# A GRU over 256 steps: state and update gate in two halves, the last two vector steps as one scan, and the candidate's bias by a product

## The chip, the cores and the metric

The kernel runs on one core of one Trainium2 chip. The metric is the device time of one execution in microseconds (us), median of the runs. Engines: TensorE (PE; PEld is its weight load), VectorE (DVE), ScalarE (ACT), GpSimd (POOL) and SyncE (SP), which here issues the DMAs.

## The reference, cut to what matters

Four layers run one after the other over x, 8 batches x 256 steps x 512 channels: two attention layers, a GRU over the 256 steps, and a last layer with a pooled term and a layer norm. The change is in the GRU, whose step is

```python
def cell(h, x):                       # h: [8, 512]
    gi = x @ W_ih + b_ih
    gh = h @ W_hh + b_hh
    i_r, i_z, i_n = jnp.split(gi, 3, axis=-1)
    h_r, h_z, h_n = jnp.split(gh, 3, axis=-1)
    r = jax.nn.sigmoid(i_r + h_r)
    z = jax.nn.sigmoid(i_z + h_z)
    n = jnp.tanh(i_n + r * h_n)
    h_new = (1.0 - z) * n + z * h
    return (h_new, h_new)
```

The bias of the candidate's recurrent part (the last third of b_hh) stands inside the product with r, so it can't be added to gi ahead of the loop as the others are. The layer's output is x plus all the states.

## The kernel before, in words

`attention_layers` (lines 6 to 640) computes the first two layers and leaves x, channels on partitions, in the SBUF tile xT [128, 4, 256, 8]. Its engines each walk through a written plan, batch by batch; batches 2 to 6 are a hardware loop (line 235), the others are unrolled.

`recurrent_and_last_layer` (line 642) has two blocks. In the first, lines 695 to 825, SP loads the weights (698 to 703). TensorE waits for all loads (793), then computes gi for all steps in 48 groups of eight 512-column products (801), and ScalarE evicts each group with the summed bias into giT (774). The candidate's recurrent bias is left out there.

Then each engine runs a loop of 128 passes with two steps in each; the steps are called u=0 and u=1. Nothing but semaphores orders the engines. The state hT has two buffers. One step is:

- TensorE: waits until the candidate's and the update gate's banks of the step before have been turned (808, 810) and giz is there (811). It puts the z part of gi into the bank of Z by products with an identity (814: 16 products). It waits for the state: at u=1 for hT itself (816), at u=0 for the sum of hT into xT (818). Then come the products of state and W_hh (823), in the order R, N, Z: for each gate 4 chunks c of the state by 4 column blocks j, so that gate block j lands on PSUM partitions 32j to 32j+7. A source product in f32 shows as two matmul instructions in the trace, so a step has 96 for the gates and 32 for giz.
- VectorE: turns R in 32x32 blocks into SBUF (742) and adds gi (744). It turns N (747), multiplies by r (750), adds rbias (753). It turns Z (756), then h-n (758), times z (761), plus n (764), which is the new hT.
- ScalarE: sigmoid for r and tanh for n (785), sigmoid for z (787), and a copy of the next pass's gi z part into giz (789).
- GpSimd: rbias = r * bias (716), plus gi's n part (718), and xT += hT (721).

The addresses of giT and xT depend on the loop's register, so an instruction that reads them has register instructions ahead of it. The second block (line 847) starts when the first is done on all engines, and is the last layer.

Of the kernel before, what the change touches and what calls it, by code (L numbers as in the profile page):

```python
# [641 lines left out]
def recurrent_and_last_layer(nc, xT, cond, w_ih, w_hh, b_ih, b_hh, wk, wo, rowc, cols, ident_in, out):  # L642

    fp32 = mybir.dt.float32
    ALU = mybir.AluOpType
# [3 lines left out]
    D = P * C  # L653
    GATES = 3
    TB = 64
    NB = 8
    RMS_EPS = 1e-6
    with ExitStack() as ctx:
        def sb(name, shape, dt=fp32):
            return ctx.enter_context(nc.sbuf_tensor(name, shape, dt))  # L660
        def pb(name, shape, dt=fp32):
            return ctx.enter_context(nc.psum_tensor(name, shape, dt))
        def sem(name):
            return ctx.enter_context(nc.semaphore(name))
        x2v = xT[:, :, :, :].rearrange("p c (i u) b -> p c i u b", u=2)
        giz = sb("giz", [P, 2, C, B])
        identz = sb("identz", [P, P])
        hT = sb("hT", [P, 2, C, B])
        bT = sb("bT", [P, 2, GATES * C])
        bsum = sb("bsum", [P, GATES * C])  # L670
        rbias = sb("rbias", [P, 2, 2, C, B])
        trn = sb("trn", [P, GATES, P])
        tr = [trn[:, g, :].rearrange("p (c m) -> p c m", c=C)[:, :, 0:B] for g in range(GATES)]
        pre = sb("pre", [P, GATES, C, B])
        act = sb("act", [P, GATES, C, B])
        tmp = sb("tmp", [P, 3, C, B])
        ps = [pb(f"gate{g}", [P, 512]) for g in range(GATES)]
        pg = [pb(f"pg{g}", [P, 512]) for g in range(4)]
        (s_ld, s_init, s_chain, s_rb, s_gi_mm, s_gi_ev, s_h, s_acc, s_giz) = (
            sem(n) for n in ("gru_loaded", "gates_cleared", "step_product", "bias_gated", "gi_products",  # L680
                             "gi_ready", "state_ready", "state_added", "giz_ready"))

        s_ps = [sem(f"gate_products{g}") for g in range(GATES)]
        s_tr = [sem(f"gate_turned{g}") for g in range(GATES)]
        s_pre = [sem(f"gate_summed{g}") for g in range(GATES)]
        s_act = [sem(f"gate_ready{g}") for g in range(GATES)]
        R, Z, N = 0, 1, 2
        NLD = 16 * 6
        MT = GATES * C
        gru = ctx.enter_context(ExitStack())  # L690
        giT = gru.enter_context(nc.sbuf_tensor("giT", [P, T + 2, GATES * C * B], fp32))
        whh = gru.enter_context(nc.sbuf_tensor("whh", [P, C, GATES * D], fp32))
        gi4 = giT[:, :, :].rearrange("p t (g c b) -> p t g c b", g=GATES, c=C)
        gi2 = giT[:, :, :].rearrange("p (i u) (g c b) -> p i u g c b", u=2, g=GATES, c=C)
        with nc.sbuf_tensor("wih", [P, C, GATES * D], fp32) as wih, nc.Block() as block:
            @block.sync
            def _(sp):
                sp.dma_start(wih[:], w_ih).then_inc(s_ld, 16)
                sp.dma_start(bT[:, 0], b_ih).then_inc(s_ld, 16)
                sp.dma_start(bT[:, 1], b_hh).then_inc(s_ld, 16)  # L700
                sp.dma_start(hT[:, 0], cond).then_inc(s_ld, 16)
                sp.dma_start(whh[:], w_hh).then_inc(s_ld, 16)
                sp.dma_start(identz[:], ident_in).then_inc(s_ld, 16)

            @block.gpsimd
            def _(pool):
                pool.wait_ge(s_ld, NLD)

                pool.sem_inc(s_tr[N], 1)
                pool.sem_inc(s_tr[Z], 1)  # L710
                bias_n = bT[:, 1, 2 * C:].rearrange("p (c a) -> p c a", a=1).to_broadcast([P, C, B])
                with pool.Fori(0, T // 2) as i:
                    for u in range(2):

                        pool.wait_ge(s_act[R], i * 2 + (u + 1))
                        pool.tensor_tensor(rbias[:, u, 0], act[:, R], bias_n, ALU.mult).then_inc(s_rb, 1)  # L716
                        pool.wait_ge(s_rb, i * 4 + (2 * u + 1))
                        pool.tensor_tensor(rbias[:, u, 1], rbias[:, u, 0], gi2[:, bass.ds(i, 1), u, N, :, :].rearrange("p i c b -> p (i c) b"), ALU.add).then_inc(s_rb, 1)
                        pool.wait_ge(s_h, i * 2 + (u + 1))
                        xt = x2v[:, :, bass.ds(i, 1), u, :].rearrange("p c i b -> p c (i b)")  # L720
                        pool.tensor_tensor(xt, xt, hT[:, (u + 1) % 2, :, :], ALU.add).then_inc(s_acc, 1)  # L721

            @block.vector
            def _(dve):
                dve.memset(giT[:, T:T + 2, :], 0.0).then_inc(s_init, 1)
                for g in range(3):
                    dve.memset(ps[g][:, 0:P], 0.0).then_inc(s_init, 1)
                dve.wait_ge(s_ld, NLD)
                dve.tensor_tensor(bsum[:, 0:2 * C], bT[:, 0, 0:2 * C], bT[:, 1, 0:2 * C], ALU.add).then_inc(s_init, 1)
                dve.tensor_copy(bsum[:, 2 * C:], bT[:, 0, 2 * C:]).then_inc(s_init, 1)  # L730
                dve.sem_inc(s_acc, 1)
                dve.wait_ge(s_gi_ev, 4 * MT)
                with dve.Fori(0, T // 2) as i:
                    for u in range(2):
                        t = i * 2
                        now = t + (u + 1)
                        h0, h1 = hT[:, u, :, :], hT[:, 1 - u, :, :]
                        def gi(g):
                            return gi2[:, bass.ds(i, 1), u, g, :, :].rearrange("p i c b -> p (i c) b")

                        dve.wait_ge(s_ps[R], now)
                        dve.transpose(trn[:, R, :], ps[R][:, 0:P]).then_inc(s_tr[R], 1)  # L742
                        dve.wait_ge(s_tr[R], now)
                        dve.tensor_tensor(pre[:, R], tr[R], gi(R), ALU.add).then_inc(s_pre[R], 1)  # L744

                        dve.wait_ge(s_ps[N], now)
                        dve.transpose(trn[:, N, :], ps[N][:, 0:P]).then_inc(s_tr[N], 1)  # L747
                        dve.wait_ge(s_tr[N], t + (u + 2))
                        dve.wait_ge(s_act[R], now)
                        dve.tensor_tensor(tmp[:, 0], tr[N], act[:, R], ALU.mult).then_inc(s_chain, 1)  # L750
                        dve.wait_ge(s_chain, t * 3 + (3 * u + 1))
                        dve.wait_ge(s_rb, t * 2 + (2 * u + 2))
                        dve.tensor_tensor(pre[:, N], tmp[:, 0], rbias[:, u, 1], ALU.add).then_inc(s_pre[N], 1)

                        dve.wait_ge(s_ps[Z], now)
                        dve.transpose(trn[:, Z, :], ps[Z][:, 0:P]).then_inc(s_tr[Z], 1)
                        dve.wait_ge(s_act[N], now)
                        dve.tensor_tensor(tmp[:, 1], h0, act[:, N], ALU.subtract).then_inc(s_chain, 1)
                        dve.wait_ge(s_chain, t * 3 + (3 * u + 2))
                        dve.wait_ge(s_act[Z], now)  # L760
                        dve.tensor_tensor(tmp[:, 2], tmp[:, 1], act[:, Z], ALU.mult).then_inc(s_chain, 1)
                        dve.wait_ge(s_chain, t * 3 + (3 * u + 3))
                        dve.wait_ge(s_acc, t + (u + 1))
                        dve.tensor_tensor(h1, tmp[:, 2], act[:, N], ALU.add).then_inc(s_h, 1)  # L764

            @block.scalar
            def _(a):

                a.wait_ge(s_init, 6)
# [7 lines left out]
                a.wait_ge(s_gi_ev, 4 * MT)  # L777
                for u in range(2):
                    a.copy(giz[:, u], gi4[:, u, Z]).then_inc(s_giz, 1)
                with a.Fori(0, T // 2) as i:  # L780
                    for u in range(2):
                        now = i * 2 + (u + 1)
# [274 lines left out]
```

## Time and profile before

| | us |
|---|---|
| median of 3 runs (2890.47 to 2893.78) | 2892.21 |
| span of the profiled execution | 2889.4 |
| PE busy | 2099.3 (73%) |
| DVE busy | 1209.9 (42%) |
| ACT busy | 968.4 (34%) |
| POOL busy | 521.1 (18%) |

The profiled execution's time apart from its span isn't listed; its span lies 2.8 us under the median of the runs. Busy time is the sum over instructions; an instruction that waits is not busy. A busy PE is not PE at its peak, since matmuls overlap and their ends are modelled. The shares are means over stages with different limits: attention lasts up to about 1473 us of the span, the gi products from 1492 to 1661, the recurrence from 1661 to 2768, and the last layer takes the rest. In a timeline row, "idle before <-releaser" is what the engine last waited for.

### The profile page before, as it was taken

To read this page: it belongs to the slowest core of one execution; us is meant where nothing else is said; L and a number is where in the kernel's file an instruction comes from. 1 tells how busy PE (TensorE), PEld (TensorE's weight loads), DVE (VectorE), ACT (ScalarE), POOL (GpSimd) and SP (SyncE) were. 2 spreads that over 40 slices of the span, in tenths; PEclk is the share of its full clock that TensorE was granted. 3 is DMA by queue.
4 is the path that set the end of the run, shared out by engine and by line. 5 is a ranking of instruction groups with operands and counts; after the bars stand their busy time and mean duration, and the time that the engine had idled before them with its cause. 6 is when DMAs were issued, how large, how long until landed. Compare 5 with 4: busy or idle time off the path is not lost. (4 is left out here: it accounts for less than half of the span.)

```text
span 2889.4 us, 91237 instructions
## 1 busy us (share of the span) xinstructions
PE 2099.3 (73%) x38252; PEld 1231.6 (43%) x38284; DVE 1209.9 (42%) x3495; ACT 968.4 (34%) x1884; POOL 521.1 (18%) x1184
## 2 busy tenths in 40 slices
PE   1556768787786868778669977777777777777754
PEld 0122223232332223233234466666666666666631
DVE  3425435443443535344300044444444444444456
ACT  1142434344352524335122233333333333333313
POOL 4012212022222202222100011111111111111102
PEclk8687889998898989899689999999999999999977
DMA  3352423435341443530220000000000000000001
GB/s 74 43 73 60 90 34 100 58 88 78 81 74 31 101 46 88 78 85 7 68 89 0 0 1 0 0 0 0 0 0 0 0 0 0 0 0 0 0 34 58
DMA packets 51980, 111.19 MB, mean 38 GB/s; under 512 B 11985, under 2 KB 38097, under 8 KB 46049
## 3 DMA queue, kind: packets, MB, share of 16 engines
q1 hardware_dynamic: 47328, 110.03, 19.5%
q0 software_dynamic: 4608, 0.60, 0.2%
q8 instruction: 26, 0.43, 0.1%
q14 instruction: 18, 0.14, 0.0%
HBM read 80.60 MB, written 29.41 MB: 38 GB/s over the span
## 5 line engine op out<-in xcount | busy, mean ns | idle before, releaser
L823 PE MATMUL gate<-whh,hT 128*8 128x128 f32 x24576 | 718.6, 273 | 134.5 <-POOL xT L721 93.9
L823 PEld LDWEIGHTS gate<-whh,hT 128*8 128x8 f32 x24576 | 644.8, 90 | 167.1 <-POOL xT L721 110.2
L394 DVE TENSOR_REDUCE mx<-MX 128x1 f32<-128x512 f32 x768 | 494.0, 686 | 474.2 <-PE MX L524 468.9
L459 ACT ACTIVATE pr<-ST 128x1024 f32<-128x1024 f32 x384 | 373.5, 1023 | 465.2 <-PE ST L547 239.1
L524 PE MATMUL MX<-K,Q 116*128 116x512 bf16 (+1 forms) x768 | 299.2, 427 | 192.6 <-DMA Q<-d_rows 102.4
L785 ACT ACTIVATE act<-pre 128x32 f32<-128x32 f32 x512 | 118.4, 231 | 727.8 <-DVE pre L744 466.8
L742 DVE STREAM_TRANSPOSE trn<-gate 128x128 f32<-128x128 f32 x256 | 81.2, 317 | 527.4 <-PE gate L823 527.4
L524 PEld LDWEIGHTS MX<-K,Q 116*128 116x128 bf16 (+1 forms) x768 | 69.0, 99 | 466.9 <-DVE mx L394 215.3
L814 PE MATMUL gate<-identz,giz 128*8 128x32 f32 x8192 | 109.8, 193 | 143.3 <-issue 142.2
L716 POOL TENSOR_TENSOR rbias<-act,bT 128x32 f32<-128x32 f32 x256 | 61.6, 241 | 723.1 <-ACT act L785 723.1
L544 PE MATMUL ST<-Q,K 119*128 119x512 bf16 x512 | 147.1, 413 | 49.4 <-DMA Q<-nmp 49.2
L801 PE MATMUL pg<-xT,wih 128*128 128x512 f32 x384 | 167.9, 601 | 19.3 <-DMA identz<-in_ident_dram 19.3
L340 POOL TENSOR_TENSOR nmp<-nm,zero 16x128 bf16<-16x128 f32 x48 | 21.4, 445 | 877.9 <-ACT nm L476 877.9
L814 PEld LDWEIGHTS gate<-identz,giz 128*8 128x8 f32 x8192 | 84.5, 89 | 210.2 <-issue 210.2
L785 ACT ACT_TABLE_LOAD x128 | 164.2, 1283 | 9.7
L546 PE MATMUL ST<-Q,K 100*128 100x512 bf16 x256 | 105.3, 412 | 69.8 <-DMA Q<-nmp 66.8
L570 PE MATMUL AV<-pr,va 128*17 128x512 f32 x1024 | 147.3, 650 | 0.4 <-ACT pr L459 0.4
L721 POOL TENSOR_TENSOR xT<-xT,hT 128x32 f32 x256 | 64.6, 252 | 364.8 <-DVE hT L764 364.8
L801 PEld LDWEIGHTS pg<-xT,wih 128*128 128x128 f32 x384 | 74.0, 193 | 112.9 <-issue 93.1
L476 ACT ACTIVATE nm<-MX 16x128 f32<-16x128 f32 x48 | 12.8, 267 | 282.3 <-PE MX L529 282.3
L747 DVE STREAM_TRANSPOSE trn<-gate 128x128 f32<-128x128 f32 x256 | 81.2, 317 | 54.9 <-PE gate L823 54.9
L544 PEld LDWEIGHTS ST<-Q,K 119*128 119x128 bf16 x512 | 51.0, 103 | 118.3 <-issue 43.6
(141 smaller groups left out, 2193.3 us busy)
## 6 DMA issues: line engine op xcount, KB each, us to landing
Q<-d_q SPq DMA_DIRECT2D x112, 256.0 KB
K<-d_k SPq DMA_DIRECT2D x112, 256.0 KB
d_q<-piece_q SPq DMA_DIRECT2D x96, 128.0 KB
d_k<-piece_k SPq DMA_DIRECT2D x96, 128.0 KB
xin<-in_x_dram SPq DMA_DIRECT2D x8, 512.0 KB, 12.7
x<-in_x_dram SPq DMA_DIRECT2D x8, 512.0 KB, 12.5
out_dram<-sq SPq DMA_DIRECT2D x4, 1024.0 KB, 4.3
wih<-in_w_ih_dram SPq DMA_DIRECT2D x1, 3072.0 KB, 9.7
```

The costliest lines, as they stand in the source:

```text
L394: dve.reduce_max(mx[:, u, 4 * i + qb:4 * i + qb + 1], banks[0][:, :], AX.X).then_inc(mx_red[u].sem, 1)
L459: act.activation(pr[:, kc % 2, 2 * p:2 * p + 2, :], ST[:, 2 * p * T:(2 * p + 2) * T].rearrange("p (a t) -> p a t", a=2), ACT.Exp, scale=SC ...
L524: pe.matmul(banks[0][:, :], q[0:r, h, tok(qb)], k[0:r, h, :], start=True, stop=True).then_inc(mx_mm[u].sem, 1)
L544: last = pe.matmul(o, K0[0:R0 + 7, h, tok(kc)], Q0[0:R0 + 7, h, :], start=True, stop=True)
L546: pe.matmul(o, K1[0][0:R1 + 4, h, tok(kc)], Q1[0][0:R1 + 4, h, :], start=True, stop=False)
L570: last = pe.matmul(AV[r, :], v, pr[:, kc % 2, i, :], start=kc == 0, stop=kc == KC - 1)
L742: dve.transpose(trn[:, R, :], ps[R][:, 0:P]).then_inc(s_tr[R], 1)
L747: dve.transpose(trn[:, N, :], ps[N][:, 0:P]).then_inc(s_tr[N], 1)
L785: a.activation(act[:, g], pre[:, g], f).then_inc(s_act[g], 1)
L801: last = pe.matmul(pg[n % 4][:, :], wih[:, k, m * P:(m + 1) * P], xT[:, k, TB * blk:TB * (blk + 1), :].rearrange("p t b -> p (t b)"), star ...
L814: pe.matmul(ps[Z][32 * j:32 * j + B, 32 * c:32 * c + 32], giz[:, u, c, :], identz[:, 32 * j:32 * j + 32], start=c == 0, stop=False)
L823: last = pe.matmul(ps[g][32 * j:32 * j + B, 0:P], hT[:, u, c, :], whh[:, c, o:o + P], start=c == 0 and g != Z, stop=c == C - 1)
```

## The change: what it does

- The state is kept as pairs, state [128, 2 buffers, 4 chunks, 8, 2]; the state is the second of each pair. Half 0 is chunks 0 and 1, half 1 is chunks 2 and 3, each with a semaphore of its own.
- The last two vector steps (times z, plus n) become one scan per half over 32 elements. A scan carries s = by * s + plus along the row. With by = (0, z) and plus = (h-n, n) the first of a pair gives h-n and the second z*(h-n)+n.
- The update gate is computed in two halves of 64 columns, in banks of their own, double-buffered by step: its products, its turn and its sigmoid are split, and half 1 follows half 0.
- TensorE begins R and N with half 0 of the state (chunks 0 and 1 of R, then of N), and goes on with half 1 (chunks 2 and 3 of R, then of N), then Z half 0 and Z half 1. It no longer waits for the sum into xT.
- The candidate's bias enters N's bank by one 128-column product in f32r of pick and bn_rows (the bias in a high part and a rest), as the first of its accumulation. The two GpSimd operations of rbias go; VectorE adds gi's n part itself.
- giz is copied by GpSimd, two steps ahead, after the products of Z half 1, instead of by ScalarE.
- A pass of the loop has four steps (64 passes). Three small loads are added, two of them after a wait of SP for a VectorE memset; a few set-up operations and a wait of TensorE for all evictions ahead of the loop are added.

The diff, cut to its core. The lines that it removes are those of the loops in the listing above (712 to 721, 733 to 764, 778 to 789, 804 to 825); they are left out here.

```diff
...
+        state = sb("state", [P, 2, C, B, 2])
+        by = sb("by", [P, C, B, 2])
+        plus = sb("plus", [P, C, B, 2])
...
+        bn = sb("bn", [64, P])
...
+        bn_rows = sb("bn_rows", [64, P], f32r)
...
+        psz = [[pg[0], pg[1]], [pg[2], pg[3]]]
...
+        def pairs(t, a):
+            return t[:, half(a)].rearrange("p c b v -> p (c b v)")
...
+                sp.dma_start(pick_ld[:], pick_in).then_inc(s_ld, 16)
+                sp.wait_ge(s_init, 1)
+                for j in range(2):
+                    sp.dma_start(bn[32 * j:32 * j + C, :], bhn_rows).then_inc(s_ld, 16)
...
             def _(pool):
...
+                pool.wait_ge(s_gi_ev, 4 * MT)
+                for u in range(2):
+                    pool.tensor_copy(giz[:, u], gi4[:, u, Z]).then_inc(s_giz, 1)
+                with pool.Fori(0, T // U) as i:
+                    for u in range(U):
+                        q = u % 2
+                        now = i * U + (u + 1)
+                        pool.wait_ge(s_psz[1], now)
+                        pool.tensor_copy(giz[:, q], gi_at(i, u + 2, Z)).then_inc(s_giz, 1)
+                        pool.wait_ge(s_h[0], i * U + (u + 2))
+                        pool.wait_ge(s_h[1], i * U + (u + 2))
+                        xt = xv[:, :, bass.ds(i, 1), u, :].rearrange("p c i b -> p c (i b)")
+                        pool.tensor_tensor(xt, xt, state[:, 1 - q, :, :, 1], ALU.add).then_inc(s_acc, 1)
...
+                dve.sem_inc(s_acc, 2)
+                for s in s_h:
+                    dve.sem_inc(s, 1)
+                for s in (s_tr, *s_trz):
+                    dve.sem_inc(s, 2)
                 dve.wait_ge(s_gi_ev, 4 * MT)
...
+                with dve.Fori(0, T // U) as i:
+                    for u in range(U):
+                        q = u % 2
+                        t = i * U
                         now = t + (u + 1)
...
+                        h0 = state[:, q, :, :, 1]
+                        dve.wait_ge(s_ps[tR], now)
+                        dve.transpose(trn[:, R, :], psR[:, 0:P]).then_inc(s_tr, 1)
+                        dve.wait_ge(s_tr, t * 2 + (2 * u + 3))
+                        dve.tensor_tensor(pre[:, 0], tr[R], gi_at(i, u, R), ALU.add).then_inc(s_pre[tR], 1)
+                        dve.wait_ge(s_ps[tN], now)
+                        dve.transpose(trn[:, N, :], psN[:, 0:P]).then_inc(s_tr, 1)
+                        dve.wait_ge(s_tr, t * 2 + (2 * u + 4))
+                        dve.wait_ge(s_r, now)
+                        dve.tensor_tensor(tmp[:], tr[N], rg[:], ALU.mult).then_inc(s_chain, 1)
+                        dve.wait_ge(s_chain, t * 2 + (2 * u + 1))
+                        dve.tensor_tensor(pre[:, 1], tmp[:], gi_at(i, u, N), ALU.add).then_inc(s_pre[tN], 1)
+                        dve.wait_ge(s_psz[0], now)
+                        dve.transpose(trn[:, Z, 0:64], psz[0][q][:, 0:64]).then_inc(s_trz[0], 1)
+                        dve.wait_ge(s_n, now)
+                        dve.tensor_tensor(plus[:, :, :, 0], h0, plus[:, :, :, 1], ALU.subtract).then_inc(s_chain, 1)
+                        dve.wait_ge(s_chain, t * 2 + (2 * u + 2))
                         dve.wait_ge(s_acc, t + (u + 1))
...
+                        dve.wait_ge(s_z[0], now)
+                        dve.tensor_tensor_scan(pairs(state[:, 1 - q], 0), pairs(by, 0), pairs(plus, 0), 0.0, ALU.mult, ALU.add).then_inc(s_h[0], 1)
+                        dve.wait_ge(s_psz[1], now)
+                        dve.transpose(trn[:, Z, 64:128], psz[1][q][:, 0:64]).then_inc(s_trz[1], 1)
+                        dve.wait_ge(s_z[1], now)
+                        dve.tensor_tensor_scan(pairs(state[:, 1 - q], 1), pairs(by, 1), pairs(plus, 1), 0.0, ALU.mult, ALU.add).then_inc(s_h[1], 1)
...
+                with a.Fori(0, T // U) as i:
+                    for u in range(U):
+                        now = i * U + (u + 1)
+                        a.wait_ge(s_pre[tR], now)
+                        a.activation(rg[:], pre[:, 0], ACT.Sigmoid).then_inc(s_r, 1)
+                        a.wait_ge(s_pre[tN], now)
+                        a.activation(plus[:, :, :, 1], pre[:, 1], ACT.Tanh).then_inc(s_n, 1)
+                        for z in range(2):
+                            a.wait_ge(s_trz[z], i * U + (u + 3))
+                            a.activation(by[:, half(z), :, 1], tr[Z][:, half(z)], ACT.Sigmoid).then_inc(s_z[z], 1)
...
+                pe.wait_ge(s_init, 12)
+                pe.wait_ge(s_gi_ev, 4 * MT)
+                def products(bank, g, q, c, first, done, cols=slice(0, P)):
+                    for j in range(4):
+                        o = g * D + P * j
+                        last = pe.matmul(bank[32 * j:32 * j + B, 0:cols.stop - cols.start], state[:, q, c, :, 1],
+                                         whh[:, c, o + cols.start:o + cols.stop], start=first, stop=done)
+                    return last
+                with pe.Fori(0, T // U) as i:
+                    for u in range(U):
+                        q = u % 2
+                        t = i * U
                         pe.wait_ge(s_giz, t + (u + 1))
...
+                        for z in range(2):
+                            pe.wait_ge(s_trz[z], t + (u + 1))
+                            for c in range(H):
+                                for j in range(4):
+                                    pe.matmul(psz[z][q][32 * j:32 * j + B, 32 * c:32 * c + 32], giz[:, q, H * z + c, :], identz[:, 32 * j:32 * j + 32], start=c == 0, stop=False)
+                        pe.wait_ge(s_tr, t * 2 + (2 * u + 2))
+                        pe.matmul(psN[:, 0:P], pick[:], bn_rows[:], start=True, stop=False)
+                        pe.wait_ge(s_h[0], t + (u + 1))
+                        for c in range(H):
+                            products(psR, R, q, c, c == 0, False)
+                        for c in range(H):
+                            products(psN, N, q, c, False, False)
+                        pe.wait_ge(s_h[1], t + (u + 1))
+                        for c in range(H, C):
+                            last = products(psR, R, q, c, False, c == C - 1)
+                        last.then_inc(s_ps[tR], 1)
+                        for c in range(H, C):
+                            last = products(psN, N, q, c, False, c == C - 1)
+                        last.then_inc(s_ps[tN], 1)
+                        for z in range(2):
                             for c in range(C):
...
+                                last = products(psz[z][q], Z, q, c, False, c == C - 1, slice(64 * z, 64 * z + 64))
+                            last.then_inc(s_psz[z], 1)
...
```

## Rows read from the trace of the kernel before

**Rows 1.** Busy time by stretch: us, PE, PEld, DVE, ACT, POOL busy (x instructions), PEclk, DMA share, GB/s.

```profile
1661.00:2768.00 1107.00, 828.20 (x32768) 729.19 (x32768) 515.41 (x2304) 368.29 (x1154) 190.95 (x768) 1.00 0.00 0
```

**Rows 2.** Timeline of two steps: start us, us, engine, line, operation, x count [idle before <-releaser].

```profile
2201.37 2.81 PE L823 MATMUL gate<-whh,hT 128*8 128x128 f32 x96 [0.32 <-DVE hT L764]
...
2205.07 1.28 ACT L785 ACT_TABLE_LOAD   x1
2205.22 0.19 DVE L764 TENSOR_TENSOR hT<-tmp,act 128x32 f32<-128x32 f32 x1
2205.60 0.25 POOL L721 TENSOR_TENSOR xT<-xT,hT 128x32 f32 x1 [1.42 <-DVE hT L764]
...
2205.90 2.81 PE L823 MATMUL gate<-whh,hT 128*8 128x128 f32 x96 [0.70 <-POOL xT L721]
2207.03 0.32 DVE L742 STREAM_TRANSPOSE trn<-gate 128x128 f32<-128x128 f32 x1 [1.62 <-PE gate L823]
2207.49 0.19 DVE L744 TENSOR_TENSOR pre<-trn,giT 128x32 f32<-128x32 f32 x1
2207.72 0.23 ACT L785 ACTIVATE act<-pre 128x32 f32<-128x32 f32 x1 [1.36 <-DVE pre L744]
2207.90 0.32 DVE L747 STREAM_TRANSPOSE trn<-gate 128x128 f32<-128x128 f32 x1 [0.21 <-PE gate L823]
...
2208.25 0.19 DVE L750 TENSOR_TENSOR tmp<-trn,act 128x32 f32<-128x32 f32 x1
...
2208.76 0.19 DVE L753 TENSOR_TENSOR pre<-tmp,rbias 128x32 f32<-128x32 f32 x1 [0.31 <-POOL rbias L718]
2208.87 0.31 DVE L756 STREAM_TRANSPOSE trn<-gate 128x128 f32<-128x128 f32 x1
2208.98 0.23 ACT L785 ACTIVATE act<-pre 128x32 f32<-128x32 f32 x1 [1.03 <-DVE pre L753]
2209.21 0.23 ACT L787 ACTIVATE act<-trn 128x32 f32<-128x32 f32 x1
2209.24 0.19 DVE L758 TENSOR_TENSOR tmp<-hT,act 128x32 f32<-128x32 f32 x1
...
2209.28 0.42 PE L814 MATMUL gate<-identz,giz 128*8 128x32 f32 x32 [0.57 <-issue]
...
2209.54 0.19 DVE L761 TENSOR_TENSOR tmp<-tmp,act 128x32 f32<-128x32 f32 x1
2209.77 0.19 DVE L764 TENSOR_TENSOR hT<-tmp,act 128x32 f32<-128x32 f32 x1
...
2210.01 2.81 PE L823 MATMUL gate<-whh,hT 128*8 128x128 f32 x96 [0.32 <-DVE hT L764]
```

**Rows 3.** Timeline, the loop's ends: first products and last VectorE operation.

```profile
1661.37 2.84 PE L823 MATMUL gate<-whh,hT 128*8 128x128 f32 x96
...
2767.04 0.19 DVE L764 TENSOR_TENSOR hT<-tmp,act 128x32 f32<-128x32 f32 x1
```

**Rows 4.** Timeline of the last layer, two VectorE operations over 512 elements.

```profile
2790.01 0.68 DVE L879 TENSOR_TENSOR kq<-keys 64x512 f32<-64x512 f32 x1
...
2825.26 3.35 DVE L931 RECIPROCAL rs<-rs 128x512 f32<-128x512 f32 x1 [4.17 <-ACT rs L997]
```

**Rows 5.** Groups by line, 1490 to 1661 us, TensorE (line, shapes, x count, busy us, mean ns).

```profile
L801 PE MATMUL pg<-xT,wih 128*128 128x512 f32 x384 | 167.9, 601 | 19.3 <-DMA identz<-in_ident_dram 19.3
```

**Rows 6.** DMA queues in 600 to 1250 us (packets, MB, share), all that moved.

```profile
q1 hardware_dynamic: 20637, 47.09, 39.9%
q0 software_dynamic: 2304, 0.30, 0.4%
```

**Rows 7.** The page's DMA queues over the whole span, the instruction queue.

```profile
q8 instruction: 26, 0.43, 0.1%
```

**Rows 8.** Busy time by stretch, 600 to 1250 us.

```profile
600.00:1250.00 650.00, 503.53 (x2458) 196.98 (x2475) 293.15 (x535) 261.52 (x311) 135.75 (x196) 0.89 0.40 73
```

**Rows 9.** Groups by line, 600 to 1250 us, VectorE (96 of these a batch).

```profile
L394 DVE TENSOR_REDUCE mx<-MX 128x1 f32<-128x512 f32 x380 | 244.3, 686 | 211.7 <-PE MX L524 210.4
```

More of the change, by code:

```diff
@@ L676, in recurrent_and_last_layer @@
[L676 to L677 removed]
+        pre = sb("pre", [P, 2, C, B])
+        rg = sb("rg", [P, C, B])
+        tmp = sb("tmp", [P, C, B])
+        ps = [pb(f"gate{g}", [P, 512]) for g in range(3)]
         pg = [pb(f"pg{g}", [P, 512]) for g in range(4)]
[L679 to L681 removed]
@@ new lines, in recurrent_and_last_layer @@
+        R, Z, N = 0, 1, 2
+        s_ps = [sem(f"gate_products{g}") for g in (R, N)]
+        s_psz = [sem(f"update_products{a}") for a in range(2)]
+        s_tr = sem("gates_turned")
+        s_trz = [sem(f"update_turned{a}") for a in range(2)]
+        s_pre = [sem(f"gate_summed{g}") for g in (R, N)]
+        s_z = [sem(f"update_ready{a}") for a in range(2)]
+        s_h = [sem(f"state_ready{a}") for a in range(2)]
+        psR, psN = ps[0], ps[1]
+        tR, tN = 0, 1
+        NLD = 16 * 9
@@ L723, in _ @@
             @block.vector
             def _(dve):
-                dve.memset(giT[:, T:T + 2, :], 0.0).then_inc(s_init, 1)
-                for g in range(3):
-                    dve.memset(ps[g][:, 0:P], 0.0).then_inc(s_init, 1)
+                dve.memset(bn[:], 0.0).then_inc(s_init, 1)
+                dve.memset(giT[:, T:T + U, :], 0.0).then_inc(s_init, 1)
+                dve.memset(psR[:, 0:P], 0.0).then_inc(s_init, 1)
+                dve.memset(by[:], 0.0).then_inc(s_init, 1)
+                dve.memset(state[:, 1], 0.0).then_inc(s_init, 1)
@@ L746, in _ @@
[L746 to L753, printed above, removed]
@@ L776, in _ @@
                                      ACT.Identity, bias=bsum[:, m:m + 1]).then_inc(s_gi_ev, 1)
[L777 to L782, printed above, removed]
-                        for g, f in ((R, ACT.Sigmoid), (N, ACT.Tanh)):
-                            a.wait_ge(s_pre[g], now)
-                            a.activation(act[:, g], pre[:, g], f).then_inc(s_act[g], 1)
-                        a.wait_ge(s_tr[Z], i * 2 + (u + 2))
-                        a.activation(act[:, Z], tr[Z], ACT.Sigmoid).then_inc(s_act[Z], 1)
-                        a.copy(giz[:, u], gi2[:, bass.ds(i + 1, 1), u, Z, :, :].rearrange("p i c b -> p (i c) b")).then_inc(s_giz, 1)
+                with a.Fori(0, T // U) as i:
[8 more added lines that the diff above has]
+                            a.activation(by[:, half(z), :, 1], tr[Z][:, half(z)], ACT.Sigmoid).then_inc(s_z[z], 1)
             @block.tensor
```

100 lines of the change are left out of this document (30 added, 70 removed).

## The prediction

> **What bounds the kernel now.** I read the windows by stage first. The change touches the stretch from 1661 to 2768 us, 1107 of 2889 us, in which TensorE is busy for 828 us, VectorE for 515 and ScalarE for 368 [rows 1]. No engine is full, no byte moves, and the clock is granted in full. So a chain from engine to engine sets this time, and the timeline of one step shows it [rows 2]. Take T = 2205.90, the first product of a step, as zero:
>
> - +1.13 turn of R, +1.59 plus gi, +1.82 sigmoid; +2.00 turn of N, +2.35 times r, +2.86 plus rbias, +3.08 tanh, +3.34 h-n, +3.64 times z, +3.87 plus n, +4.11 next step's first product.
>
> The 96 matmuls last 2.81 with a last one of 0.273, so one starts each 26.7 ns: 0.213 us for a gate and chunk (8 matmuls), 0.853 for a gate. R turned at +1.13 is 0.853 + 0.28; N at +2.00 is 1.706 + 0.29. So N's turn is set by TensorE, and from there VectorE and ScalarE set all. R has some slack, and Z's products and turn are covered. The other step is longer: from 2201.37 to 2205.90 it takes 4.53, because L823 waits there for xT's sum (L764 at 2205.22, L721 at 2205.60, L823 at 2205.90: 0.68) and not for the state (2209.77 to 2210.01: 0.24). A pair takes 8.64, a step 4.32, and 255 of them with one step's tail make the 1105.7 us from 1661.37 to 2767.04 [rows 3].
>
> **The parts, on the path.** The unit is one step; T is now the first product on half 0.
>
> 1. TensorE doesn't wait for the sum: 0.44 at every other step, -0.22 a step. The sum moves past the next step's start; the scan waits for the one of two steps before, done long ago.
> 2. R is ready later. R's second half comes behind N's first: 6 chunks of products instead of 4, 1.28 instead of 0.853. Turn of R at +1.56, plus gi +2.02, sigmoid +2.25. N is ready at +2.00 as before, but VectorE takes it behind R's sum: +2.13, done +2.45. "Times r" now waits for the sigmoid. From ScalarE's start to VectorE's the rows show 0.26 (tanh to h-n) and 0.33 (sigmoid z to times z) [rows 2]; I take 0.30: +2.55 instead of +2.35. Cost +0.20.
> 3. rbias goes. "Plus rbias" came 0.51 after "times r", with 0.31 idle on GpSimd. The new sum reads giT, so it is a dependent VectorE operation (0.23, L761 to L764) plus register work for the address: L742 to L744 takes 0.46 where L747 to L750 takes 0.35, so 0.11. 0.34 instead of 0.51: -0.17. Sum at +2.89, tanh +3.11, h-n +3.37.
> 4. One scan for two operations. h-n to times z was 0.30, times z to plus n 0.23, plus n to product 0.24, of which 0.19 is the operation. Now the scan starts 0.30 behind h-n, +3.67; its z was turned at +3.00 beside the tanh, and its sigmoid follows the tanh at +3.34, 0.33 ahead of the scan. Its length has no row. Below: 0.19, a plain operation over 32 elements. Above: per element the reciprocal's 3.35 us for 512 [rows 4], 0.19 + 32 x 5.5 ns = 0.36. I take 0.225, since it does two dependent operations on each element and a plain one costs 1.02 ns for each (0.68 us for 512 against 0.19 for 32, rows 2 and 4): nearer to the plain row. Next step's first product: +3.67 + 0.225 + 0.05 = **+3.94**. Against 4.11 this is -0.23 + 0.03 for the scan and rounding.
> 5. Half 1 behind it: turn of Z half 1 at +3.81. It is 0.065 shorter than 0.309 (64 columns less at 1.02 ns), done +4.05; sigmoid +4.09, scan +4.42, half ready for TensorE at +4.70. That is 0.76 after the next step's start, and half 0 has work for 0.853. So it costs nothing, with 0.09 to spare; what it exceeds 0.853 by goes onto the step in full.
>
> So a step takes 3.94, against 4.32. I read from this that halving the state buys nothing (it moves R back) and that the gain comes from parts 1, 3 and 4.
>
> **Covered, at zero.** Z's 64 matmuls of 64 columns: 32 columns start each 7.3 ns (L814: 0.42 for 32, the last 0.19), 128 each 26.7, so 64 at 13.4 are 0.855 for Z as before. TensorE ends the gates at +2.56, giz at about +3.0. The bias product is one matmul 128 wide; the nearest row, with four times the columns, has 0.60 [rows 5], and there are 0.94 until +3.94. Without that cover it would cost up to 0.6 a step. Its wait, both turns of this step, ends at +2.45, ahead of the giz products. GpSimd's giz copy waits for Z half 1's products (+2.84) and has more than a step until its use; behind it in the queue is only the sum into xT, for which VectorE waits two steps later. It may meet VectorE at the SBUF (about +3.0 to +3.25, against plus gi at +2.89): between 0 and 0.1 a step; in rows 2 VectorE's operations have 0.19 beside GpSimd's too, so 0. The table load (1.28) stands behind the last sigmoid of a pass, now +4.32 to +5.60; the next sigmoid is due at 3.94 + 2.25 = +6.19.
>
> **Once.** From +4.42 instead of +3.87 in the last step, inside the sum below. giz by GpSimd and the wait for all evictions ahead of the loop: +0.3 (the copy waited for them before, too). Three loads of 32 KB and less behind identz, the last one waited for (19.3 us, rows 5): between 0 and +3, I take +1; SP's wait is for a VectorE memset at the block's start, with two small loads behind it.
>
> **The sum.** 255 x 3.94 + 4.42 = 1009.1; 1105.7 - 1009.1 = 96.6 less, 1.3 more: -95.3. The profiled execution's span of 2889.4 becomes 2794; it lies 2.8 under the median of the runs, so 2892.2 becomes **2797**.
>
> **Loading of the code, a rule against it.** A pass on TensorE grows from 512 matrix instructions (256 matmuls, 256 weight loads) to 4 x 322 = 1288. The first layers' loop shows what such a pass costs: from 600 to 1250 us TensorE ran 4933 of them [rows 8], with 380 maxima at 96 a batch [rows 9], 1246 per pass, and no packet of an instruction queue moved in four passes [rows 6], while over the span there were 26 of 16 KB [rows 7]. So a pass of this size stays loaded, and I put it at zero. The Trainium skill (Runtime: NRT & Kernel Launch, Instruction fetch mechanics) says that a taken branch whose target is outside a window of two pages of 256 instructions forces a fetch before execution goes on. By it this loop would stall at each of its 64 jumps. The trace disagrees for a loop of 1246.
>
> **Rivals.**
> - *Half 1 comes late.* If the scan takes 0.36, or the four handoffs after it 0.05 more each, half 1 comes 0.85 to 0.95 after half 0, and TensorE stands still between R's halves. For it: only 0.09 to spare, and a scan's length counts twice. Against it: each handoff is from a row. Price: 0.1 to 0.3 a step with the longer scan, 26 to 77 us: 2823 to 2874.
> - *Slower: the code is fetched at every jump.* The place is TensorE's jump, each 4 steps. The 26 pieces took 0.1% of 16 engines' 2889 us, 46 us, so about 1.8 us each (rounded, 0.9 to 2.7). It decides from 97 / 64 = 1.5 us a pass; at 1.8 the time is 2797 + 115 = 2912, more if several pieces are waited for. For it: the pass is 2.5 times longer, and some 4% above the one that stayed loaded. Against it: rows 6 to 9.
> - *More than forecast.* R to N tighter than I have it (0.26 for 0.30), the scan at 0.19 and started 0.04 sooner: 3.83 a step, 2768; less only if R's lateness doesn't count, down to 2745.
> - *The rearrangement does nothing:* all of 1, 3 and 4 would have to be covered by something else. Nothing in rows 2 runs beside them. 1 in 100.
>
> **Chances.** Forecast 0.67 (2766 to 2835, its unknowns added up), half 1 late 0.20, below 2766 0.05, no change 0.01, code 0.07. The range takes in the forecast and most of the late half: 2764 to 2852. Outside are the worst of the late half, the code and a little below. Faster by over 0.2% (6 us, about what a measurement of this kernel can tell from no change) 0.92, same 0.01, slower 0.07.
>
> **What would show it.** The step's period in the timeline: 3.94, and the same for all four u (before 4.53 and 4.11). L823's successors wait for VectorE's scan, never for GpSimd. R's turn 1.56 and N's 2.13 after the first product, times r 0.3 after the sigmoid's start, tanh at +3.11. Scan rows of about 225 ns; of 360 they make the rival. No idle of TensorE ahead of R's chunks 2 and 3; idle there is the late half. No instruction-queue packets between 1700 and 2660 us. The last layer unchanged at 121 us. Wrong would be a period over 4.1, or idle time of TensorE once each four steps.

## The result and the profile after

The changed kernel takes 2798.52 us (median of 4 runs, 2796.64 to 2799.49), the kernel before 2891.34 in the same comparison: ratio 0.968, 95% interval 0.9666 to 0.9694, 93 us less. Forecast were 2797 and a range of 2764 to 2852.

The busy time by stretch, columns as in [rows 1]:

```profile
1665.00:2676.00 1011.00, 869.44 (x41216) 807.37 (x41216) 528.66 (x2560) 293.43 (x1088) 118.65 (x514) 1.00 0.00 0
```

The stretch of the loop is 96 us shorter, though PE is busy for 869 us of 1011 where it was for 828 of 1107, with 8448 more matmul instructions: its idle time fell from 279 to 142 us. The clock is again granted in full. One step in the timeline, the answer to [rows 2]:

```profile
2207.32 1.94 PE L843 MATMUL gate<-whh,state 128*8 128x128 f32 x64 [0.58 <-DVE state L797]
...
2207.69 0.23 DVE L801 TENSOR_TENSOR_SCAN state<-by,plus 128x32 f32<-128x32 f32 x1 [0.29 <-ACT by L822]
...
2208.88 0.32 DVE L778 STREAM_TRANSPOSE trn<-gate 128x128 f32<-128x128 f32 x1 [0.96 <-PE gate L843]
...
2209.34 0.19 DVE L780 TENSOR_TENSOR pre<-trn,giT 128x32 f32<-128x32 f32 x1
2209.45 0.31 DVE L783 STREAM_TRANSPOSE trn<-gate 128x128 f32<-128x128 f32 x1
2209.57 0.23 ACT L817 ACTIVATE rg<-pre 128x32 f32<-128x32 f32 x1 [1.91 <-DVE pre L780]
2209.90 0.19 DVE L786 TENSOR_TENSOR tmp<-trn,rg 128x32 f32<-128x32 f32 x1
...
2210.23 0.19 DVE L788 TENSOR_TENSOR pre<-tmp,giT 128x32 f32<-128x32 f32 x1
...
2210.34 0.21 POOL L741 COPY giz<-giT 128x32 f32 x1 [1.93 <-PE pg L843]
...
2210.35 0.33 PE L858 MATMUL gate<-bn_rows,pick 64*128 64x128 f32 x1
2210.46 0.23 ACT L819 ACTIVATE plus<-pre 128x32 f32<-128x32 f32 x1 [0.66 <-DVE pre L788]
2210.62 0.22 ACT L822 ACTIVATE by<-trn 128x16 f32<-128x16 f32 x1
2210.72 0.19 DVE L793 TENSOR_TENSOR plus<-state,plus 128x32 f32<-128x32 f32 x1
2210.96 0.23 DVE L797 TENSOR_TENSOR_SCAN state<-by,plus 128x32 f32<-128x32 f32 x1
...
2211.24 1.93 PE L843 MATMUL gate<-whh,state 128*8 128x128 f32 x64 [0.57 <-DVE state L797]
```

Read from T = 2207.32: R's turn +1.56, its sum +2.02, sigmoid +2.25, N's turn +2.13, times r +2.58, N's sum +2.91, tanh +3.14, h-n +3.40, first scan +3.64, next product +3.92. Both TensorE waits for a state name the scan of half 0 (L797), none names GpSimd, here and in the whole stretch from 1700 to 2660 us. Half 1's scan starts 0.37 behind the product that half 0 released. The bias product (L858) is done at +3.36, with 0.56 to spare; GpSimd's giz copy stands at +3.02 to +3.23 beside a turn that reads PSUM.

The loop's ends, from the same timeline of the changed kernel, the answer to [rows 3]. First its start:

```profile
1665.84 1.94 PE L843 MATMUL gate<-whh,state 128*8 128x128 f32 x64
...
1674.45 1.70 PE L843 MATMUL gate<-whh,state 128*8 128x128 f32 x53
...
1677.39 0.50 PE L843 MATMUL gate<-whh,state 128*8 128x128 f32 x10 [1.24 <-issue]
...
1681.24 1.38 PE L843 MATMUL gate<-whh,state 128*8 128x128 f32 x43 [0.69 <-issue]
...
1684.71 1.93 PE L843 MATMUL gate<-whh,state 128*8 128x128 f32 x64 [0.23 <-DVE state L797]
```

And its end, the last half of the state:

```profile
2675.28 0.23 DVE L801 TENSOR_TENSOR_SCAN state<-by,plus 128x32 f32<-128x32 f32 x1 [0.28 <-ACT by L822]
```

From 1665.84 to 2675.28 there are 1009.4 us, where 1009.1 were forecast and 1105.7 were before. The four steps of the first pass take 18.87, from then on a step takes 3.93 (251 x 3.93 = 986, and 18.87 make the 1005.1 to the last step's start at 2670.98). So the first pass costs 3.2 once. Its five gaps name "issue"; the middle ones stand 126 or 127 weight loads apart, so the 644 of the pass are some 5 pieces, and 5 packets of the instruction queue moved between 1660 and 1700 us. I read from this that the body is loaded there.

The loop starts 4.5 us later than before. TensorE's set-up makes 0.7 of it (1.3 were forecast): 0.4 more wait for the loads and 0.3 more from the first gi product to the loop. The other 3.8 come from the attention layers, which the change doesn't touch and which ended later in this profiled execution. The last layer takes the 122 us that it took. So the span is 91.7 us shorter, where 95.3 were forecast: the loop alone gave 96.2, forecast 96.6.

### The profile page after: what moved, and what is told of

The parts are those of the page before. It is cut to its first block and busy times, and to the rows that moved or that the text cites. A ratio compares the mean times of both kernels' runs of the same rounds, so it can differ in the third digit from the quotient of the medians.

```text
span 2797.7 us, 107154 instructions
## 1 busy us (share of the span) xinstructions
PE 2145.9 (77%) x46732; PEld 1309.5 (47%) x46732; DVE 1224.2 (44%) x3757; ACT 892.7 (32%) x1818; POOL 448.3 (16%) x930
## 5 line engine op out<-in xcount | busy, mean ns | idle before, releaser
L843 PE MATMUL gate<-whh,state 128*8 128x128 f32 x16384 | 496.1, 273 | 126.1 <-DVE state L797 124.2
L843 PEld LDWEIGHTS gate<-whh,state 128*8 128x8 f32 x16384 | 421.4, 90 | 162.8 <-DVE state L797 159.9
L843 PE MATMUL pg<-whh,state 128*8 128x64 f32 x16384 | 276.6, 219 | 1.4 <-issue 1.4
L778 DVE STREAM_TRANSPOSE trn<-gate 128x128 f32<-128x128 f32 x256 | 81.2, 317 | 418.1 <-PE gate L843 418.1
L843 PEld LDWEIGHTS pg<-whh,state 128*8 128x8 f32 x16384 | 256.8, 90 | 1.8 <-issue 1.8
L817 ACT ACTIVATE rg<-pre 128x32 f32<-128x32 f32 x256 | 58.6, 229 | 404.5 <-DVE pre L780 404.5
L834 PE MATMUL pg<-xT,wih 128*128 128x512 f32 x384 | 167.8, 600 | 19.7 <-DMA bn<-in_bhn_rows_dram 19.7
L822 ACT ACTIVATE by<-trn 128x16 f32<-128x16 f32 x512 | 111.8, 218 | 136.3 <-DVE trn L799 135.8
L745 POOL TENSOR_TENSOR xT<-xT,state 128x32 f32 x256 | 64.8, 253 | 388.0 <-DVE state L801 388.0
L856 PE MATMUL pg<-identz,giz 128*8 128x32 f32 x8192 | 114.7, 193 | 12.8 <-issue 11.6
L819 ACT ACTIVATE plus<-pre 128x32 f32<-128x32 f32 x256 | 59.4, 232 | 171.0 <-DVE pre L788 171.0
```

The lines of the kernel that those rows point to most:

```text
L745: pool.tensor_tensor(xt, xt, state[:, 1 - q, :, :, 1], ALU.add).then_inc(s_acc, 1)
L778: dve.transpose(trn[:, R, :], psR[:, 0:P]).then_inc(s_tr, 1)
L822: a.activation(by[:, half(z), :, 1], tr[Z][:, half(z)], ACT.Sigmoid).then_inc(s_z[z], 1)
L834: last = pe.matmul(pg[n % 4][:, :], wih[:, k, m * P:(m + 1) * P], xT[:, k, TB * blk:TB * (blk + 1), :].rearrange("p t b -> p (t b)"), star ...
L843: last = pe.matmul(bank[32 * j:32 * j + B, 0:cols.stop - cols.start], state[:, q, c, :, 1], whh[:, c, o + cols.start:o + cols.stop], start ...
L856: pe.matmul(psz[z][q][32 * j:32 * j + B, 32 * c:32 * c + 32], giz[:, q, H * z + c, :], identz[:, 32 * j:32 * j + 32], start=c == 0, stop=F ...
```

## The experiments

All edits but one are to the changed kernel. Times are medians of 4 or 5 runs where a ratio stands beside them, else one run. The kernel before ran beside each; its medians were 2885 to 2891. The attention layers end at other times in each profiled execution, whatever was edited: the first gi product starts between 1491.6 and 1498.9 us. So a few us between single runs say nothing, and where it matters I give the loop's own length, from its first gate product to its last VectorE operation: 1105.7 before, 1009.4 in the changed kernel.

**The whole state.** The bank pairs of Z become one bank for each parity.

```diff
+                        dve.transpose(trn[:, Z, :], psz[q][:, 0:P]).then_inc(s_trz, 1)
...
+                        dve.tensor_tensor_scan(pairs(state[:, 1 - q]), pairs(by), pairs(plus), 0.0, ALU.mult, ALU.add).then_inc(s_h, 1)
...
-                        pe.wait_ge(s_h[0], t + (u + 1))
...
+                        pe.wait_ge(s_h, t + (u + 1))
+                        for c in range(C):
+                            last = products(psR, R, q, c, c == 0, c == C - 1)
+                        last.then_inc(s_ps[tR], 1)
...
```

> The changed kernel with the state and the update gate whole again: products in the order R, N, Z once the whole state is there, one turn and one sigmoid of Z, one scan over 64 elements; all the rest of the change stays. Theory (halving buys nothing and makes R late): R's turn comes back to 1.13 us after the first product, times r to 2.35, h-n to about 3.17, the scan starts at 3.43 and is some 0.29 long instead of 0.225; a step takes 3.78 instead of 3.93, so about 38 us less than the changed kernel, 2760. Rival (the early start with half 0 is what the change gains): TensorE now starts only where half 1 was ready, about 0.6 later, and a step grows to 4.2 or more, 2870 or later.

2795.72 us, ratio 0.9672 (0.9654 to 0.9691): neither. It is level with the changed kernel; the loop takes 1006.6, and a step 3.93 as there. Its timeline says why:

```profile
2202.11 1.94 PE L836 MATMUL gate<-whh,state 128*8 128x128 f32 x64 [0.60 <-DVE state L795]
...
2203.24 0.32 DVE L776 STREAM_TRANSPOSE trn<-gate 128x128 f32<-128x128 f32 x1 [1.18 <-PE gate L836]
...
2203.86 1.06 PE L836 MATMUL pg<-whh,state 128*8 128x128 f32 x32
...
2204.46 0.19 DVE L784 TENSOR_TENSOR tmp<-trn,rg 128x32 f32<-128x32 f32 x1
...
2204.98 0.32 DVE L789 STREAM_TRANSPOSE trn<-pg 128x128 f32<-128x128 f32 x1
...
2205.28 0.19 DVE L791 TENSOR_TENSOR plus<-state,plus 128x32 f32<-128x32 f32 x1
2205.33 0.23 ACT L815 ACTIVATE by<-trn 128x32 f32<-128x32 f32 x1
2205.69 0.29 DVE L795 TENSOR_TENSOR_SCAN state<-by,plus 128x64 f32<-128x64 f32 x1 [0.22 <-ACT by L815]
...
2206.04 1.94 PE L836 MATMUL gate<-whh,state 128*8 128x128 f32 x64 [0.60 <-DVE state L795]
```

R's turn is at +1.13 and times r at +2.35, as the theory had it, and h-n at +3.17. But the scan starts at +3.58, not 3.43. It waits for Z's sigmoid, which started at +3.22: Z's last product ends at +2.81, its turn starts at +2.87 and is 128 wide (0.32), and the sigmoid follows it. So a new wait takes the place of R's. This accounts for about a third of the 0.15: from the tanh's start to h-n there are 0.26 here, from this sigmoid's start to the scan 0.36, and what makes it 0.10 longer stays open. The halves do buy something: half of Z is turned and through the sigmoid in time. In the changed kernel that gain and R's delay would then cancel, which the next run tests.

**R earlier.** If so, there should be an order with both. Only TensorE's order changes:

```diff
-                        for c in range(H):
-                            products(psN, N, q, c, False, False)
+                        products(psN, N, q, 0, False, False)
                         pe.wait_ge(s_h[1], t + (u + 1))
...
-                        for c in range(H, C):
+                        for c in range(1, C):
                             last = products(psN, N, q, c, False, c == C - 1)
```

> The changed kernel with another order of TensorE alone: chunks 0 and 1 of R and only chunk 0 of N, then, with half 1, chunks 2 and 3 of R and chunks 1 to 3 of N. The same products. Theory (R's late turn costs 0.2 a step, and half 1 comes 0.66 after half 0): R is done at 1.09 instead of 1.28, its turn starts at 1.37 instead of 1.56, times r at 2.39 instead of 2.58, with N's turn at 2.00; a step takes 3.74 instead of 3.93, so 48 us less than the changed kernel, 2750. Idle of TensorE between the halves is about 0.02. Rival (N's products or half 1 set the step, not R's lateness): no difference, 2798.

2742.13 us, ratio 0.9489 (0.9471 to 0.9507), 56 us less than the changed kernel (the loop 953.2, 56 less too); 48 were expected.

```profile
2203.19 1.94 PE L843 MATMUL gate<-whh,state 128*8 128x128 f32 x64
...
2203.56 0.22 DVE L801 TENSOR_TENSOR_SCAN state<-by,plus 128x32 f32<-128x32 f32 x1 [0.29 <-ACT by L822]
...
2204.53 0.32 DVE L778 STREAM_TRANSPOSE trn<-gate 128x128 f32<-128x128 f32 x1 [0.75 <-PE gate L843]
...
2205.19 0.32 DVE L783 STREAM_TRANSPOSE trn<-gate 128x128 f32<-128x128 f32 x1
...
2205.55 0.19 DVE L786 TENSOR_TENSOR tmp<-trn,rg 128x32 f32<-128x32 f32 x1
...
2206.90 1.83 PE L843 MATMUL gate<-whh,state 128*8 128x128 f32 x60 [0.35 <-DVE state L797]
```

R's turn is at +1.34, N's at +2.00, times r at +2.36 with both its inputs just there, the next product at +3.71. Half 1 came at 0.65 (its scan at +0.37, and 0.28 from a scan's start to a product), where R's half and a chunk of N are 0.64 of work. With R early the step in halves takes 3.71, the step with the whole state 3.93: that difference is what the halves are worth in this order.

**No chunk of N ahead of half 1.**

```diff
-                        for c in range(H):
-                            products(psN, N, q, c, False, False)
                         pe.wait_ge(s_h[1], t + (u + 1))
...
-                        for c in range(H, C):
+                        for c in range(C):
                             last = products(psN, N, q, c, False, c == C - 1)
```

> The run with R earlier, but no chunk of N ahead of half 1: chunks 0 and 1 of R, then, with half 1, chunks 2 and 3 of R and all of N. Theory (half 1 comes 0.65 after half 0, and TensorE can then only stand still): 0.43 of work for 0.65, so 0.22 idle between the halves; R's turn stays at 1.34 us, but N's comes at 2.22 instead of 2.00, times r at 2.57, a step is 3.92: 2796, as slow as the changed kernel although R is early. Rival (only R's lateness costs, N has slack): 2742 as in the run with R earlier.

2791.76 us (2796 were expected); the loop takes 1004.2, a step 3.91. The weight loads show the stop, and N's turn comes late:

```profile
2202.14 0.34 PEld L843 LDWEIGHTS gate<-whh,state 128*8 128x8 f32 x16 [0.49 <-DVE state L797]
...
2202.79 1.21 PEld L843 LDWEIGHTS gate<-whh,state 128*8 128x8 f32 x48 [0.31 <-DVE state L801]
...
2203.48 0.32 DVE L778 STREAM_TRANSPOSE trn<-gate 128x128 f32<-128x128 f32 x1 [0.75 <-PE gate L843]
...
2204.36 0.32 DVE L783 STREAM_TRANSPOSE trn<-gate 128x128 f32<-128x128 f32 x1 [0.22 <-PE gate L843]
```

R's turn at +1.34, N's at +2.22. The first 16 weight loads end their 0.43 of work, and the next wait until +0.65 for L801. So 0.22 of lateness beyond the work in hand cost 0.20 a step here, about 1 to 1, as the rival "half 1 comes late" was priced, and one chunk of N (0.21) is what fills the gap.

**The single parts.** No wait for the sum, in the kernel before (the counts of s_h go up by one with it, which isn't shown here):

```diff
-                        if u == 1:
-                            pe.wait_ge(s_h, t + 1)
-                        else:
-                            pe.wait_ge(s_acc, t + 1)
+                        pe.wait_ge(s_h, t + (u + 1))
```

> The kernel before, with one edit: TensorE waits for the new state at both steps, nowhere for the sum into xT. Theory (part 1 of the prediction): the step of 4.53 becomes 4.11 like the other, 128 times 0.42 to 0.44, so 55 us less than the kernel before, 2837. Rival (something else is due at that place, loop overhead of an engine for one): the two steps stay apart, at most half of that, 2865 or more.

2839.74 us, 50 less than the kernel before beside it (2890.03). The loop itself takes 1048.2, 57.5 less, which is the 55 to 56 expected; the attention layers ended later in this execution. Both steps are now 4.09 to 4.10, and both wait for hT:

```profile
2202.62 2.81 PE L821 MATMUL gate<-whh,hT 128*8 128x128 f32 x96 [0.32 <-DVE hT L765]
...
2206.71 2.81 PE L821 MATMUL gate<-whh,hT 128*8 128x128 f32 x96 [0.26 <-DVE hT L765]
...
2210.81 2.81 PE L821 MATMUL gate<-whh,hT 128*8 128x128 f32 x96 [0.32 <-DVE hT L765]
```

Two operations for each scan:

```diff
-                        dve.tensor_tensor_scan(pairs(state[:, 1 - q], 0), pairs(by, 0), pairs(plus, 0), 0.0, ALU.mult, ALU.add).then_inc(s_h[0], 1)
+                        dve.tensor_tensor(tmz[:, half(0)], plus[:, half(0), :, 0], by[:, half(0), :, 1], ALU.mult).then_inc(s_gi_mm, 1)
+                        dve.wait_ge(s_gi_mm, t * 2 + (4 * MT + 2 * u + 1))
+                        dve.tensor_tensor(state[:, 1 - q, half(0), :, 1], tmz[:, half(0)], plus[:, half(0), :, 1], ALU.add).then_inc(s_h[0], 1)
```

> The changed kernel with each scan put back into two operations of 16 elements per lane (times z, then plus n), in both halves. Theory (part 4): the product's operand is ready one dependent operation later: times z at 3.64 us after the first product, plus n 0.21 later, next step 0.22 after that, 4.08 instead of 3.93, so 38 us more than the changed kernel, 2837. Half 1 then comes 0.82 after half 0, still inside 0.853. Rival (the scan saves nothing, as it is itself longer): 2798 to 2805. Second rival (half 1 now comes too late and TensorE stops between the halves): 2860 or more.

2836.48 us, 38 more than the changed kernel (the loop 1050.2, 41 more). The first of the two starts 0.24 behind h-n, the second 0.21 later, the product 0.23 after that.

rbias back on GpSimd, and no bias product (the candidate's products start their own accumulation):

```diff
+                        pool.wait_ge(s_r, now)
+                        pool.tensor_tensor(rbias[:, q, 0], rg[:], bias_n, ALU.mult).then_inc(s_gi_mm, 1)
+                        pool.wait_ge(s_gi_mm, i * (2 * U) + (4 * MT + 2 * u + 1))
+                        pool.tensor_tensor(rbias[:, q, 1], rbias[:, q, 0], gi_at(i, u, N), ALU.add).then_inc(s_gi_mm, 1)
...
-                        pe.matmul(psN[:, 0:P], pick[:], bn_rows[:], start=True, stop=False)
```

> The changed kernel without the bias product: GpSimd again makes r times bias plus gi's n part from the reset gate, and VectorE waits for it before it adds it. Theory A (a wait costs what it is late in this order): in the kernel before the sum came 1.04 us after the reset gate's sigmoid began; here the sigmoid begins at 2.25, so the sum comes at 3.29 instead of 2.91, 0.38 a step, 97 us more than the changed kernel, 2895. Theory B (part 3 of the prediction is worth 0.17 wherever it stands): 43 us more, 2842.

2907.5 us, 109 more (the loop 1119.3, 110 more): later than the kernel before. Theory A, and 12 beyond it. The timeline:

```profile
2204.48 0.23 ACT L824 ACTIVATE rg<-pre 128x32 f32<-128x32 f32 x1 [2.00 <-DVE pre L786]
2204.78 0.24 POOL L742 TENSOR_TENSOR rbias<-rg,bT 128x32 f32<-128x32 f32 x1 [1.54 <-ACT rg L824]
2204.81 0.26 DVE L792 TENSOR_TENSOR tmp<-trn,rg 128x32 f32<-128x32 f32 x1
...
2205.49 0.19 DVE L795 TENSOR_TENSOR pre<-tmp,rbias 128x32 f32<-128x32 f32 x1 [0.41 <-POOL rbias L744]
```

From the reset gate's sigmoid to N's sum (L795) there are 1.01, where the changed kernel has 0.66. That is 0.35 of the 0.43 a step. Most of the rest lies between the scan and the next product, 0.37 instead of 0.28 (scan at 2214.95, product at 2215.32, and so in the steps beside it); what makes it longer stays open. Times r (L792) takes 0.26 instead of 0.19 beside GpSimd's operation; the sum waits for GpSimd even so.

**The length of the pass.** `U = 4` becomes `U = 8`, and in another run `U = 2`.

> The changed kernel with eight steps in a pass of the loop instead of four, 32 passes: 2576 matrix instructions in a pass on TensorE instead of 1288, nothing else. Theory (a pass stays loaded up to some size above 1288 that no run has shown): if 2576 still fits, 2798 as before and no packet of an instruction queue in the loop. Rival (the Trainium skill's 2048 instructions of TensorE's instruction memory and its fetch at a jump): packets of 16 KB in every pass; if only the jump waits, one piece of about 1.8 us in each of 32 passes, 58 us more, 2856; if they are read ahead in time, packets but no time.

3187.44 us, 389 more than with four steps, far beyond the 58 of the rival. The DMA queues between 1700 and 2660 us, where before and after nothing moved:

```profile
q8 instruction: 262, 4.29, 1.9%
q14 instruction: 1, 0.01, 0.0%
```

And who waited for whom, of TensorE's weight loads in that stretch (us in total, times, longest):

```profile
PEld pg L856 <- issue: 169.4, 66, 4.0
PEld gate L843 <- issue: 74.0, 84, 1.4
```

The groups that name "issue" are the largest; it is time in which TensorE waited for nothing that the profile shows, and its own instructions are what is left. 389 us in 32 passes are 12.2 a pass. At 8 x 3.93 + 12.2 = 43.6 us a pass, the 960 us hold 22 passes, and 262 packets are 12 for each. The packets are of 16 KB (4.29 MB over 262). In one pass looked at closely, one wait of 3.65 us stands at its start, the others are of 0.5 to 2.5 us inside it, most of them 127 weight loads apart, so some 254 matrix instructions. This is the rival that the prediction gave 7 in 100 for four steps, except that it placed the wait at the jump alone. Between 1288 and 2576 no run was made.

The Trainium skill (Runtime: NRT & Kernel Launch, Instruction fetch mechanics) gives TensorE room for 2048 instructions, filled first in, first out in pieces of 256. Its 256 agree with the 254 between two gaps; by it, an estimate, the 2576 matrix instructions are 10 pieces, where 12 packets are seen, and what the others carry isn't shown. Its room lies between the two sizes run here, so it agrees with both, but no run tells it from another limit between them. By its window of two pieces the pass of 1288 would have been fetched anew as well; the trace disagrees.

> The changed kernel with two steps in a pass of the loop instead of four, as the kernel before had. Theory (loop control and table load run while the engines wait for each other; below the size where the code is fetched again, the length of a pass costs nothing): 2798, within 4 us. Rival (the longer pass is part of the gain): 2 to 15 us more.

2798.82 us, as with four (the loop 1007.8, within 2 us). The longer pass gains nothing and lies nearer to the size that is fetched anew.

**gi at a fixed address**, on top of R earlier:

```diff
-                        pool.tensor_copy(giz[:, q], gi_at(i, u + 2, Z)).then_inc(s_giz, 1)
+                        pool.wait_ge(s_pre[tN], now)
+                        pool.tensor_copy(gis[:, q].rearrange("p g c b -> p (g c b)"), gia[:, bass.ds(i + (u + 2) // U, 1), (u + 2) % U, :].rearrange("p i e -> p (i e)")).then_inc(s_giz, 1)
...
-                        dve.tensor_tensor(pre[:, 1], tmp[:], gi_at(i, u, N), ALU.add).then_inc(s_pre[tN], 1)
+                        dve.tensor_tensor(pre[:, 1], tmp[:], gis[:, q, N], ALU.add).then_inc(s_pre[tN], 1)
```

> The run with R earlier, and GpSimd copies all three gates' gi of a step (96 elements instead of 32), two steps ahead, to a tile with a fixed address; VectorE reads R's and N's part from there, so it has no register work ahead of its two sums. GpSimd waits for the step's last sum before it copies. Theory (0.11 of register work stands ahead of each sum, on the path): plus gi of R 0.10 earlier, but N's turn at 2.00 sets times r at 2.35 as before; the sum of N follows 0.23 after times r instead of 0.33. 0.10 a step, 26 us less than the run with R earlier: 2716. Rival (GpSimd's longer copy delays a VectorE operation, or the register work ran beside the wait): 2735 to 2745.

2726.66 us, ratio 0.9443 (0.9427 to 0.9459): 15 less than R earlier (the loop 13 less), where 26 were expected. The sum does follow 0.23 behind times r. But h-n takes 0.27 instead of 0.19:

```profile
2205.34 0.26 POOL L744 COPY gis<-giT 128x96 f32 x1 [1.94 <-PE pg L846]
2205.38 0.27 DVE L796 TENSOR_TENSOR plus<-state,plus 128x32 f32<-128x32 f32 x1
...
2205.68 0.22 DVE L800 TENSOR_TENSOR_SCAN state<-by,plus 128x32 f32<-128x32 f32 x1
```

**The copy behind the sum into xT**, on top of that (the two waits ahead of the copy go, and the copy stands as the last line of the step):

> The run with gi at a fixed address, and GpSimd's 96-element copy moved behind its sum into xT, so that it runs at the start of the next step, where VectorE stands idle; its two waits fall away. Theory (in that run h-n takes 0.27 instead of 0.19 because GpSimd's copy runs beside it): h-n 0.19 again, the step 3.57 instead of 3.65, 20 us less: 2706. Rival (0.27 has another cause, its operands' addresses for one): 2727 as before, h-n still 0.27.

2712.91 us, ratio 0.9379 (0.9363 to 0.9395), 14 less again and 86 less than the changed kernel. The groups by line, VectorE, of the run before this and of this one:

```profile
L796 DVE TENSOR_TENSOR plus<-state,plus 128x32 f32<-128x32 f32 x241 | 66.5, 276 | 33.0
```

```profile
L794 DVE TENSOR_TENSOR plus<-state,plus 128x32 f32<-128x32 f32 x239 | 46.3, 194 | 32.8
```

0.276 against 0.194 for the same operation: GpSimd's copy beside it was the cause. The steady step is 3.59, where 3.57 was expected: of the 20 us 6 are missing. In one step of four the products start 0.29 to 0.31 behind the scan instead of 0.28; that is too little to make up the 6, and the rest stays open.

## Why the prediction was right, and where it was not

The forecast was right, in sum and in the step: 3.94 forecast, 3.93 steady and 1009.4 us for the loop against 1009.1. That the loop agrees to 0.3 us is in part luck: small misses in the parts and in the first pass, below, went against each other.

- Part 1 (no wait for the sum, 0.22 a step, 56 us): the loop is 57.5 us shorter by it alone, the run 50.
- Part 2 (R late, 0.20): times r at +2.58, forecast +2.55. Shown from the other side: R earlier alone takes 56 us away.
- Part 3 (rbias, 0.17): the sum came 0.33 behind times r (0.34 forecast). But what this part is worth depends on the order around it: taken back alone it costs 109 us, 0.43 a step. GpSimd starts when the reset gate's sigmoid is there, which the change made late; in the kernel before it started while N was being turned. The forecast could use 0.17 because it went along the path once, with R moved and rbias gone together. Taken back one by one the parts give other numbers.
- Part 4 (the scan): 0.225 forecast, 0.225 measured (225 ns over 245). It starts 0.24 behind h-n and not 0.30; the chain up to h-n came 0.03 later than forecast, so half of that is lost again. Taken back it costs 38 us, the number expected. The reason for its length (two operations in series for each element) was only argued.
- Part 5 (half 1): forecast 0.76 behind half 0, measured 0.65, mostly since the handoffs from turn to sigmoid to scan took 0.51 and not 0.61. No idle time between the halves: the 64 weight loads run through in 1.65.
- The step that failed is the reading behind part 5: "halving the state buys nothing (it moves R back)". With the halves undone the time is the same, not 38 us less. I had Z's turn and sigmoid as covered, and for a whole Z they aren't once R is early: h-n moves forward to +3.17 and Z's sigmoid isn't there. With half of Z they are covered, and R early takes 56 us off. Nothing of it was in the sum, so the number held.
- Covered work: the bias product at no cost, done 0.56 ahead; giz copy and table load too. But the reason given for the copy beside VectorE at no cost, that [rows 2] show 0.19 beside GpSimd, doesn't hold: in that step no VectorE operation on SBUF alone ran beside a GpSimd one for more than 0.02. The copy fell beside a turn that reads PSUM and cost nothing there; where one started with h-n, h-n took 0.08 longer. The loads: TensorE waited 19.7 us for them, before 19.3 [rows 5]; 0.4 instead of 1.
- The code: no instruction packets between 1700 and 2660 us, so the reading of [rows 6 to 9] held for 1288. Where it ends is not shown, only that it is below 2576. The 3.2 us of the first pass were not forecast; the 0.01 by which the step was put too long made up for them (255 x 0.01 = 2.6).

## What to carry to other kernels

Where a chain through several engines sets the time, write down for one period when each input of each joint is there: the worth of a part is read from the joint that it ends in, and changes as soon as the other input moves. When work comes in two halves, count the work in hand until the second one arrives and put first what is on the longest way from there. This kernel's loop on TensorE has a size from which its code is fetched anew in every pass: twice the unroll cost 14%, and half of it cost nothing. Look for instruction packets inside a loop before unrolling it further.

## What the runs showed of the hardware that was not expected

- A TensorE loop of 2576 matrix instructions fetched its code in every pass, 12 packets of 16 KB and 12.2 us; one of 1288 or 644 fetched nothing between 1700 and 2660 us. The price is not that of the jump alone (3.65 us in the pass looked at) but of gaps all through the pass.
- A VectorE operation with two SBUF inputs took 0.26 to 0.28 instead of 0.19 us when a GpSimd operation started within 0.04 us of it (L792 beside L742, L796 beside L744), whether GpSimd copied or multiplied. Where it started 0.09 or more after GpSimd's it kept 0.19, though GpSimd was still at work (L795 beside L746 in the run with rbias back, h-n beside the giz copy in the run with R earlier; GpSimd's spans are rough). Turns from PSUM (0.24) beside a GpSimd copy stayed as they were.
- The half sigmoid behind the tanh (L822 behind L819) started 0.16 after it; in [rows 2] the whole one started 0.23 after. No run tells why.
